# The first layer norm's 1/sqrt(variance + eps): from one GpSimd power to a ScalarE square root and a VectorE reciprocal

## The reference

```
def _layernorm(x, axis=-1, eps=1e-05):
    m = jnp.mean(x, axis=axis, keepdims=True)
    v = jnp.var(x, axis=axis, keepdims=True)
    return (x - m) / jnp.sqrt(v + eps)
...
    x = L0_attn_x
    x = _layernorm(x + _L0_attn_ref(x, L0_attn_Wq, L0_attn_Wk, L0_attn_Wv, L0_attn_Wb, L0_attn_conv_q, L0_attn_conv_k, L0_attn_conv_v, L0_attn_g, L0_attn_Wo), axis=-1)
    x = _layernorm(x + _L0_ffn_ref(x, L0_ffn_gate_w, L0_ffn_gate_bias, L0_ffn_Wg, L0_ffn_Wu, L0_ffn_Wd, L0_ffn_Sg, L0_ffn_Su, L0_ffn_Sd), axis=-1)
```

## Time and profile before

| | |
|---|---|
| time of the kernel before, median of 3 runs | 899.36 us (898.68 to 899.79) |
| the profiled execution: its own time, its span | 898.73 us, 896.9 us |
| busy: PE, DVE, ACT, POOL | 718.8, 503.3, 314.9, 562.3 us |
| norm powers on POOL (L390) | 24, 24.2 us busy |
| stage 1 until the last scatter is issued, stage 2, stage 3 | about 450, 385 and 62 us |

### The profile page before, as it was taken

The page is one execution under the profiler, slowest core; times in us unless marked ns, Lnnn a source line. Parts: engine busy times, 40 slices in busy tenths (PEclk is TensorE's granted clock), DMA queues, the critical chain, the costliest instruction groups (busy, mean ns, idle before and its releaser), DMA issues.

```text
span 896.9 us, 17331 instructions
## 1 busy us (share of the span) xinstructions
PE 718.8 (80%) x5078; PEld 621.5 (69%) x5078; DVE 503.3 (56%) x1682; ACT 314.9 (35%) x843; POOL 562.3 (63%) x574
## 2 busy tenths in 40 slices
PE   5789898989898978675989788888898799771385
PEld 3677686767676857443579788888897699760384
DVE  2457878898888887664355343434434333430274
ACT  2233232323232422120356445445454544430022
POOL 0000477777777776767717777777777777777341
PEclk9889898999898989696999979879889987995599
DMA  7203041414242322115345544443444444411695
GB/s 188 81 1 94 29 149 60 150 59 150 73 137 82 116 89 74 62 53 143 91 118 145 126 114 111 106 117 98 103 112 114 107 113 113 106 34 33 255 408 193
DMA packets 96606, 101.10 MB, mean 113 GB/s; under 512 B 22312, under 2 KB 80414, under 8 KB 96515
## 3 DMA queue, kind: packets, MB, share of 16 engines
q1 hardware_dynamic: 72035, 61.56, 24.8%
q0 software_dynamic: 21504, 36.75, 12.2%
q10 hardware_dynamic: 2976, 1.69, 0.7%
HBM read 56.14 MB, written 45.88 MB: 114 GB/s over the span
## 4 chain that ended last, share of the span: by engine, by line
PE 23%; POOL 22%; DVE 21%; issue 20%; DMA 10%; ACT 1%; SPq 1%; POOLq 1%; ACTq 0%; DVEq 0%
POOL y_dram L418 17%; DMA y_dram<-arena 6%; POOL rows_dram L399 5%; DMA arena<-y_dram 3%; PE fc L1040 3%; PE fa L1040 2%; PE pa L1065 2%; PE fb L1040 2%; PE ba L1045 2%; PE pb L1065 2%; DVE arena L675 2%; PE bb L1040 1%; DVE arena L988 1%; DVE arena L679 1%; PE pb L1045 1%
## 5 line engine op out<-in xcount | busy, mean ns | idle before, releaser
L418 POOL DMA_INDIRECT y_dram<-arena x288 | 282.0, 979 | 105.2 <-issue 79.6
L399 POOL DMA_INDIRECT rows_dram<-rows x256 | 255.8, 999 | 98.4 <-issue 77.5
L390 POOL TENSOR_TENSOR rstd<-var_eps,minus_half 128x2 f32<-128x2 f32 (+1 forms) x24 | 24.2, 1007 | 123.3 <-DVE var_eps L617 123.3
L574 ACT ACTIVATE arena<-weights 128x176 f32 x384 | 99.5, 337 | 0.9
L988 DVE TENSOR_TENSOR arena<-bb,arena 128x512 f32<-128x512 f32 x36 | 24.9, 692 | 104.3 <-DMA y_dram<-arena 98.3
L1254 PE MATMUL bb<-weights,arena 88*128 x384 | 55.0, 295 | 30.5 <-DVE arena L1013 15.3
L988 DVE TENSOR_TENSOR arena<-ba,arena 128x512 f32<-128x512 f32 x36 | 24.9, 692 | 91.9 <-DMA y_dram<-arena 91.4
L1254 PEld LDWEIGHTS bb<-weights,arena 88*128 88x128 f32 x384 | 49.7, 206 | 34.5 <-issue 34.5
L1254 PE MATMUL ba<-weights,arena 88*128 x384 | 56.0, 299 | 19.2 <-DVE arena L1013 11.9
L1254 PEld LDWEIGHTS ba<-weights,arena 88*128 88x128 f32 x384 | 51.1, 210 | 23.1 <-issue 23.1
L1040 PE MATMUL fb<-arena 128*128 128x128 f32 x384 | 52.8, 280 | 12.3 <-DVE arena L675 12.0
(11 more groups left out here) (252 smaller groups left out, 1489.6 us busy)
## 6 DMA issues: line engine op xcount, KB each, us to landing
arena<-y_dram SPq DMA_DIRECT2D x16, 1024.0 KB, 12.1
arena<-rows_dram SPq DMA_DIRECT2D x192, 76.0 KB
weights<-experts SPq DMA_DIRECT2D x16, 608.0 KB
arena<-rows_dram SPq DMA_DIRECT2D x192, 38.0 KB
y_dram<-arena POOLq DMA_INDIRECT x288
rows_dram<-rows POOLq DMA_INDIRECT x256, 2.3
rows_dram<-zero SPq DMA_DIRECT2D x8, 304.0 KB, 7.1
xc<-x_chan SPq DMA_DIRECT2D x8, 256.0 KB, 4.0
```

Of the source, the lines that this page charges most:

```text
L390: pool.tensor_tensor(rstd[b % 2][:, 0:tiles], var_eps[b % 2][:, 0:tiles], minus_half[:, 0:tiles], ALU.pow).then_inc(S.rstd_done, 1)
L399: pool.indirect_dma_start(rows_dram, bass.IndirectOffsetOnAxis(ap=slot_of(a)[:, i, k:k + 1], axis=0), rows[:, NT * a + i, :], None).then_i ...
L418: pool.indirect_dma_start(y_dram, bass.IndirectOffsetOnAxis(ap=go_to[:, t:t + 1], axis=0), y_sb[q % YRING][:, i, :], None, bounds_check=B ...
L574: ins = act.activation(w_here[q % 2][:, (2 * i + h) * 2 * I:(2 * i + h + 1) * 2 * I], weights[:, bass.ds(at[i], 2 * I)], ACT.Copy)
```

## The change

For the eight norms of stage 1, POOL's power goes. ACT takes the square root of variance + eps into a new tile, deviation, and DVE its reciprocal just ahead of the shift. DVE's addition of eps (L617) goes too, since ACT adds eps as a bias. The second norm keeps the power on POOL.

```
             def inverse_std(b, tiles):
-                pool.wait_ge(S.ve_done, b + 1)
+                pool.wait_ge(S.ve_done, b - B + 1)
...
-            for _, a, n in sorted([(a * CYCLE + AT["rstd"], a, -1) for a in range(B)]
-                                  + [(a * CYCLE + at, a, n) for a in range(B) for n, at in enumerate(SPREAD)]):
-                if n < 0:
-                    inverse_std(a)
-                else:
-                    scatter(a, n)
+            for _, a, n in sorted((a * CYCLE + at, a, n) for a in range(B) for n, at in enumerate(SPREAD)):
+                scatter(a, n)
...
+                if op == "rstd":
+                    act.wait_ge(S.mv_done, a + 1)
+                    act.activation(deviation[n][:, :], mean_var[n][:, :, 1], ACT.Sqrt, bias=eps[:, 0:1]).then_inc(S.dev_done, 1)
...
                 ins.then_inc(S.mv_done, 1)
+                if b < B:
+                    return
...
             def shifted(b, tiles=NT):
+                if b < B:
+                    dve.wait_ge(S.dev_done, b + 1)
+                    dve.reciprocal(rstd[b % 2][:, :], deviation[b % 2][:, :]).then_inc(S.rstd_done, 1)
```

More of the change, by code:

```diff
@@ L125, in block_program @@
         share = sb("share", [P, P])
-        minus_half, half = sb("minus_half", [P, NT]), sb("half", [P, 1])
+        deviation = [sb(f"deviation{n}", [P, NT]) for n in range(2)]
+        minus_half, half, eps = sb("minus_half", [P, NT]), sb("half", [P, 1]), sb("eps", [P, 1])
         zero = sb("zero", [P, RW])
@@ L218, in block_program @@
             sx_done sd_mm ksd_done osd_done y_done tr_mm u_done o_done osq_done t_done orms_done orr_done on_done
-            ont_mm ont_done res_mm wo_mm st_done mv_done ve_done rstd_done nmr_done x1_done x1t_mm x1t_done
+            ont_mm ont_done res_mm wo_mm st_done mv_done ve_done dev_done rstd_done nmr_done x1_done x1t_mm x1t_done
             logit_mm route_step tanh_done score_done
@@ L387, in _, with inverse_std @@
         def _(pool):
-            def inverse_std(b, tiles=NT):
-                pool.wait_ge(S.ve_done, b + 1)
+            def inverse_std(b, tiles):
+                pool.wait_ge(S.ve_done, b - B + 1)
                 pool.tensor_tensor(rstd[b % 2][:, 0:tiles], var_eps[b % 2][:, 0:tiles], minus_half[:, 0:tiles],
@@ L402, in _ @@
             pool.memset(minus_half[:, :], -0.5)
+            pool.memset(eps[:, :], LN_EPS)
             pool.memset(half[:, :], 0.5).then_inc(S.half_set, 1)
```

## The result

The change took 907.35 us in the median of 6 runs (903.01 to 908.09), the kernel before 899.58 beside it (898.62 to 901.34): a ratio of 1.006 with a 95% interval of 1.0034 to 1.0085. The forecast was 903.9, so the way was right and the time lies in the stated range. The medians lie 7.8 us apart, more than the 4.5 of the sum; the ratio makes it 5.4 us, and its interval, 3.1 to 7.6, takes in the 4.5. The profiled execution took 905.70 with a span of 903.8, 6.9 above that of before.

A forecast was written before the change was run, and what follows sets the result against it. PE, nearly full, and the gapless chain through its logits to DVE were taken to bound the cycle; 2.6 + 0.6 + 1.3 = 4.5 us took the profiled 898.73 to 903.2, plus 0.63 gives 903.9 us, range 900.6 to 910.

The forecast's parts named there:

- the 4.5 of the sum: Slots of sequence 7 were to come 4.5 us later, from 2.6 + 0.6 + 1.3, moving the end of stage 1.
- the first of each pair: Load ahead of each square root in sequences 0 to 6: lies in ACT's idle time and costs nothing.
- POOL's emptier list: End of stage 1: removing eight powers from POOL was worth at most 0.05 us.
- the faster shift: First norm, sequence 1: the shift starts 0.40 us earlier, but in front of a load, so no step gives faster slots.
- The rival of a switch that costs two loads: Each exposed load costs 1.28 us more because ACT must empty first: 16.0 us in all, 915.4; chance 0.10.
- the term of 2.6 us: Sequences 0 to 5: PE waits at the logits behind the second load, 4 x 0.5 + 2 x 0.3 us.
- the term of 0.6: Sequence 6: load ahead of the router's tanh makes it 1.0 us late, up to 0.5 comes back; 0.6 taken.
- the term of 1.3: Sequence 7: both loads in the open, so x1t_c, logits, tanh, routing and slots come 1.3 us later.
- the clock rival: PE's clock falls in the new waits; half of eight places lose 1 us each, 4 more, 908; chance 0.05.
- The rival of a wait that is taken up: PE's wait at the logits is absorbed later; the 3.2 us of sequences 0 to 6 vanish, 900.7; chance 0.12.

The follow-up runs named there:

- experiments 1: The change with ScalarE's Sqrt replaced by Identity, so no table loads are needed: 899.97 us, ratio 0.9995 to the kernel before.
- experiment 2: The kernel before, POOL's power still in use, with ScalarE's square root added and its result unread (same 17 loads): 906.21 us, ratio 1.0057.
- the second profile of the change: The change measured once more, unaltered, beside more runs of the kernel before: 907.22 us against 900.15, ratio 1.006.
- the filled change: The change with five unread products ahead of each of PE's two waits behind the scan: 897.77 us, ratio 0.9960 to the kernel before.
- experiment 3: The change for sequence 7 alone, POOL's power kept for sequences 0 to 6: 902.52 us, ratio 1.0012 to the kernel before.
- 4, loads in 0 to 6: The change for sequences 0 to 6, POOL's power kept for sequence 7: 903.64 us, ratio 1.0029 to the kernel before.
- the filled pair: The kernel before and the change, each with five unread products ahead of each of PE's two waits behind the scan: 894.36 and 897.77 us.
- the one of 1163.97: One of the six runs of experiment 2, at a granted clock of 0.55, left outside its ratio: 1163.97 us.
- The pair with seven products: Seven unread products ahead of each wait: kernel before 891.91 us, ratio 0.9879; the change only on the low-clock chip, 1286.9 us.
- experiment 8: The change plus an unread Silu and Sqrt behind x1 of sequences 0 to 5, two more exposed loads each: 934.35 us, ratio 1.0358 to the kernel before.

## Why the prediction was right, and what it mis-sized

**The cause and the way.** That the loads decide, that the first of each pair is hidden in sequences 0 to 6, that POOL's emptier list gains next to nothing, and that the faster shift gains nothing were all borne out, by experiments 1 and 2 and by POOL's 5.54 us of idle time. The list was worth 0.3 us and not at most 0.05: POOL followed the slots by 0.81 us (414.50 to 415.31), not by the 0.98 read at sequence 0, so before the change its backlog was the later of the two.

**The price of a load.** 1.28 us with 0.01 to 0.02 around it, behind running activations too. The rival of a switch that costs two loads (0.10) falls. This is where ScalarE: Activation LUTs of the Trainium skill, section "What ACT_TABLE_LOAD costs", spoke against the row: its 1283 ns agree, and its drain of some 1380 ns shows at none of the loads here.

**Sequences 0 to 5, the term of 2.6 us.** Mis-sized: PE waited 0.22 at the logits of sequences 1 to 5 (1.1 us in five waits), so some 1.3 in six. I had put instructions end to end: the reciprocal started before L685 had ended (123.51 against 123.61), and x1t_c before the Tanh had (127.22 against 127.34). The shift came 0.71 us behind the moments, not 0.97, and the logits 4.18 behind the shift, not 4.23. Sequences 3 and 4 were not special, since POOL's late answer had gone with POOL's power.

**Sequence 6, the term of 0.6.** Right. The logits of the change and, behind the load, their tanh:

```profile
350.54 1.06 PE L1155 MATMUL br<-router_w,arena 128*128 128x64 f32 x8
351.36 1.28 ACT L510 ACT_TABLE_LOAD   x1
352.65 0.38 ACT L510 ACTIVATE arena<-br 128x256 f32<-128x256 f32 x1
```

The tanh starts 2.11 us behind the logits, 1.10 before (346.43 to 347.53), so 1.0 late. Against the slots of sequence 5, which came 4.64 later than before, the logits came 4.11 later and the slots of sequence 6 5.27: 0.5 came back and 0.6 was lost.

**Sequence 7, the term of 1.3.** The wait was 1.44. What I had not added was 0.8 for the logits at the lower clock (1.94 us; 1.96 and 1.97 in the second profile of the change and in experiment 2, 1.10 in the filled change, which has the same two loads).

**The sum.** The waits are thus 1.3 + 0.6 + 1.4 = 3.3 us, near the 3.5 of experiments 3 and 4 and the 3.4 of the filled pair, whose intervals are wide. In the lengths of the cycles they are 2.9. The 7.26 us of the slots in the profiled pair come out as 0.90 of the start, 0.23 at sequence 0's norm, 0.65 in the cycles of sequences 1 to 5 outside the stretches (PE had waited 1.1, so 0.4 of it was taken up), 0.59 at sequence 6, 1.45 of waiting and 0.81 at the logits of sequence 7, and 2.63 in all seven stretches together. The sum of 4.5 was 1.2 too high for the mechanism that it described (1.6 by the cycles), and 3.3 below the 7.8 of the medians. That the time still lies near it is in part luck: the two errors have opposite signs.

**The step that failed** is the clock rival, to which I gave 0.05, on the argument that waits of 0.3 to 1.3 us would not set off a fall where a cycle already had waits of half a microsecond at 0.92. The 0.92 was a mean over a cycle that has a fall in it. Two parts of that cycle of before:

```profile
143.30:157.30 14.00, 10.92 (x57) 8.98 (x56) 11.09 (x32) 4.42 (x9) 10.73 (x11) 0.76 0.17 59
157.30:187.00 29.70, 27.76 (x185) 22.38 (x184) 25.07 (x100) 9.66 (x23) 22.22 (x23) 1.00 0.39 129
```

In the new waits themselves the rival's doubt was right for sequences 0 to 6, whose logits kept the higher level (1.06 to 1.11 us); only those of sequence 7 fell, for 0.8. What it left out is that the falls already there can get longer. The profiled executions, with "rest" for the five cycles of sequences 1 to 5 outside the stretches (us):

| | first moments | six stretches | rest |
|---|---|---|---|
| before | 77.80 | 79.1 | 152.4 |
| 1, no loads | 78.78 | 79.4 | 152.2 |
| the change | 78.70 | 82.0 | 153.1 |
| the change again | 79.21 | 81.9 | 153.1 |
| 4, loads in 0 to 6 | 80.27 | 82.1 | 153.3 |
| 2, loads beside POOL's power | 79.99 | 78.1 | 157.5 |
| 3, loads in 7 only | 80.68 | 83.6 | 151.8 |

With the change's handover and loads the stretches are 2.5 to 3.0 us longer than without the loads. But experiment 2 has the loads and short falls, and experiment 3 has none in these cycles and the longest, so the loads alone don't set the length. By the medians 3.7 of the 7.1 us go when PE's waits behind the scan are filled in both kernels (by the ratios 3.1 of 5.4), so a part of the loss hangs on the falls; its size is uncertain by some 2 us. What stays open is what sets the length of a fall, and why a change at the norm lengthens those 10 us later. Open is also what sets apart the slowest runs of a kernel. The change's runs at 905.7 to 908.1 are not simply the ten runs of before at 904.4 to 907.2 with the waits added, which would lie higher. And the profiled executions of experiments 2, 3, 4 and 7, each the slowest of its kernel but for the one of 1163.97, had their first moments at 79.86 to 80.68, where before had 77.80: 2 to 3 us of the spread arise ahead of any norm. The pair with seven products, which should have shown the waits alone, has only its one half on a comparable chip.

**The rival of a wait that is taken up** (0.12) falls by the eighth experiment, where 3.0 us more in each of six cycles cost 26 or 27 us, more than their sum. Of the small waits of the change itself a share was taken up, 0.4 of 1.1 us.

## What to carry to other kernels

Before moving a small function to ScalarE, list the functions that stand before and behind it: a function of another table costs a load on the way in and one on the way back, and of the two only the one that lies in idle time is free. When an engine sits on the chain with no gap, a wait behind such a load passes on whole, in every cycle, as the 3.0 us of experiment 8 did (of waits of 0.22 us a part was taken up). Where PE has waits between bursts of small products, look at the granted clock stretch by stretch, not over a cycle: filling the waits was worth 1.2% here, more than the change lost, though it cost 2.6% on the chip whose clock was held down. And before two profiles are compared, look at how far apart they are ahead of the first changed instruction: here it was 0.9 to 2.9 us.

## What was not expected of the hardware

At the same place of each cycle PE drops from 2.4 to 1.2 GHz, and stays there for different times: a stretch of the same work took 12.7 us at a granted clock of 0.87, 13.4 to 14.4 at 0.75 or 0.76, and 12.4 at 1.00 with extra products in it. Fourteen products without use for each sequence (seven ahead of each wait, 1.72 and 1.81 us of PE's time in the trace) made the program 9 us faster. And one chip ran all kernels with PE at a granted clock of 0.76 to 0.80, a third slower (1214.6 us for the kernel before); the order of the kernels was not the same there.
